# Last stage of an attention and expert-layer kernel: weight loads ahead of the wait for gathered rows, scatters at earlier counts, a small product ahead of a large one

## What is computed

```python
gates = softmax(h @ wg.T);  w_topk, idx_topk = top_k(gates, 8);  w_topk /= w_topk.sum(-1)
rank  = position of the assignment among those of its expert;  valid = rank < 160
buf[e, rank] = h[token]                                # 64 x 160 x 256
x1, x2 = split(buf @ expert_w1.T)                      # 2 x 768 columns
out   = (x1 * silu(x2)) @ expert_w2.T                  # 64 x 160 x 256
y     = where(valid, out[e, rank] * w_topk, 0)
combined = zeros.at[token].add(y)
x = x + gb * (shared_out + combined)
```

## Time and profile before

| | us |
|---|---|
| median of 3 runs | 1895.24 |
| lowest and highest | 1889.76, 1904.81 |
| the profiled execution | 1886.24 |
| its span, first to last instruction | 1884.5 |
| PE busy in the span | 1830.4 (97%) |
| DVE, ACT, POOL busy | 1232.2, 955.2, 945.7 |

### The profile page before, as it was taken

How to read it: one execution, slowest core, us unless ns; L and a number is a source line. 1 busy time by engine, 2 the same in 40 slices (tenths; PEclk the granted TensorE clock), 3 DMA queues, 4 the chain that set the end, 5 groups by cost and what they waited for, 6 DMA issues and landing times.

```text
span 1884.5 us, 36384 instructions
## 1 busy us (share of the span) xinstructions
PE 1830.4 (97%) x12428; PEld 1612.8 (86%) x12428; DVE 1232.2 (65%) x2454; ACT 955.2 (51%) x1789; POOL 945.7 (50%) x667
## 2 busy tenths in 40 slices
PE   7999999999999999999999999998999999999995
PEld 5888888888888888677888878898999999999994
DVE  8877777777777777666776668744555555555552
ACT  6666666666666665545453354333344444444341
POOL 5666566666666665025666656654333333323234
PEclk9999999999999999999999999999999999999998
DMA  6211111111111100302111002267888888888883
GB/s 228 68 38 38 34 37 34 34 37 34 37 34 47 41 31 21 130 20 69 45 46 46 20 25 66 68 207 236 280 288 284 291 283 262 285 290 283 284 280 86
DMA packets 141016, 234.08 MB, mean 124 GB/s; under 512 B 24756, under 2 KB 88971, under 8 KB 140816
## 3 DMA queue, kind: packets, MB, share of 16 engines
q1 hardware_dynamic: 116368, 220.50, 33.9%
q0 software_dynamic: 24576, 12.69, 4.5%
HBM read 194.58 MB, written 78.45 MB: 145 GB/s over the span
## 4 chain that ended last, share of the span: by engine, by line
PE 48%; DMA 6%; issue 2%; DVE 2%; POOL 1%; ACT 0%; POOLq 0%; SPq 0%; DVEq 0%; ACTq 0%
PE bank L85 24%; PE bank L1898 19%; DMA out_rows<-c_y_rest,c_token_rest 4%; PE bank L1165 4%; DMA c_w<-in_e1T 1%; POOL out_rows L2072 1%; PE bank L2120 1%; DMA slots<-last_row,last_index 1%; PE bank L1664 1%; POOL slots L1859 0%; DVE early L1543 0%; DVE b_h_low L1446 0%; ACT b_h_high L1343 0%; PE bank L2131 0%; DMA c_x<-slots 0%
## 5 line engine op out<-in xcount | busy, mean ns | idle before, releaser
L1898 PE MATMUL bank<-c_xT,c_w 128*128 128x160 f32 x3072 | 429.9, 299 | 6.1 <-DMA c_w<-in_e1T 5.4
L1898 PEld LDWEIGHTS bank<-c_xT,c_w 128*128 128x128 f32 x3072 | 419.3, 190 | 7.4 <-DMA c_w<-in_e1T 6.4
L1859 POOL DMA_INDIRECT slots<-b_row,b_index x224 | 249.5, 1114 | 199.8 <-issue 115.6
L2072 POOL DMA_INDIRECT out_rows<-c_y,c_x x64 | 100.0, 1563 | 377.6 <-DMA out_rows<-c_y_rest,c_token_rest 230.1
L2020 DVE TENSOR_TENSOR c_gT<-bank,c_sil 128x480 f32<-128x480 f32 x128 | 84.2, 658 | 220.5 <-PE bank L1898 220.5
L1988 ACT CAST c_gTs_high<-c_gT 128x384 fp32r<-128x384 f32 x128 | 65.5, 512 | 136.1 <-DVE c_gT L2020 136.1
L1981 ACT ACTIVATE c_sil<-bank 128x480 f32<-128x480 f32 x128 | 73.1, 571 | 113.1 <-PE bank L1898 113.1
L2013 DVE TENSOR_TENSOR c_gTs_low<-c_gT,c_gTs_high 128x384 fp32r<-128x384 f32 x128 | 71.6, 559 | 74.5 <-ACT c_gTs_high L1988 73.4
L454 POOL TENSOR_TENSOR last_row<-last_row,a_e 128x256 f32<-128x256 f32 x33 | 54.4, 1648 | 127.6 <-DVE a_e L710 125.9
L85 PE MATMUL bank<-c_w2s_high,c_gTs_high 128*128 128x256 f32 x384 | 115.3, 300 | 0.9 <-DVE c_gTs_low L2013 0.9
L85 PE MATMUL bank<-c_w2s_low,c_gTs_high 128*128 128x256 f32 x384 | 108.4, 282 | 0.0
(11 more groups left out here) (329 smaller groups left out, 5457.7 us busy)
## 6 DMA issues: line engine op xcount, KB each, us to landing
c_w<-in_e1T SPq DMA_DIRECT2D x64, 1536.0 KB, 7.0
c_w<-in_e2T SPq DMA_DIRECT2D x48, 768.0 KB, 8.8
early<-in_e2T SPq DMA_DIRECT2D x16, 768.0 KB, 8.8
slots<-a_fill SPq DMA_DIRECT2D x16, 642.0 KB, 3.7
c_x<-slots SPq DMA_DIRECT2D x64, 160.5 KB, 8.5
a_x_in<-in_x SPq DMA_DIRECT2D x32, 128.0 KB, 2.0
xT_tiles<-a_xT SPq DMA_DIRECT2D x32, 128.0 KB, 1.7
swaT_tiles<-a_swaT SPq DMA_DIRECT2D x32, 128.0 KB
```

The lines of the kernel that those rows point to most:

```text
L1859: pool.indirect_dma_start(out=T["slots"], out_offset=bass.IndirectOffsetOnAxis(ap=index[:, t, k:k + 1], axis=0), in_=row[:, t, :], in_offs ...
L1898: return nc.tensor.matmul(out, lhsT, rhs, start=first, stop=last, skip_group_check=True)
L2072: pool.indirect_dma_start(out=T["out"], out_offset=bass.IndirectOffsetOnAxis(ap=token, axis=0), in_=rows, in_offset=None, bounds_check=las ...
```

## The change

On SP, the first and second weights of the experts 2 to 7 (and the second weights of expert 1) are issued before the waits for `level{n}` and `held{n}`, and so ahead of these experts' rows. In the loop and the last eight steps the order stays. On POOL, levels 4 to 7 wait for other counts. On PE, `down_rest` goes ahead of `down` in the step, and gets the waits for `gT` and `w2_low` that it needs there. On DVE, `rest_rows` and `y_rows` of the very last step change places.

```diff
+        def load_weights(n, q):
+
+            sp.wait_ge(S("h_mm"), (n - 1) * 4)
+            load_w1(sp, n, q % 2)
+
         def step(n, q, i):
             first = isinstance(n, int) and n < RING
             if first:
+                if n >= 2:
+                    load_weights(n, q)
+                if n >= 1:
+                    load_w2(sp, n, q)
                 sp.wait_ge(B(f"level{n}"), 16 * TPC)
                 if n >= HELD:
                     sp.wait_ge(B(f"held{n}"), 16 * TPC)
...
-            if not first or n >= 2:
-
-                sp.wait_ge(S("h_mm"), (n - 1) * 4)
-                load_w1(sp, n, q % 2)
-            if not first or n >= 1:
-                if not first:
-                    wait_past(sp, S("rest_mm"), quad_of(q, i) - 1)
+            if not first:
+                load_weights(n, q)
+                wait_past(sp, S("rest_mm"), quad_of(q, i) - 1)
                 load_w2(sp, n, q)
...
         g_low(E - 1, RING - 1, 1)
+        rest_rows(E - QUAD, 1, QUADS, range(2, QUAD))
         y_rows(E - 1, RING - 1)
-        rest_rows(E - QUAD, 1, QUADS, range(2, QUAD))
...
-        level(4, "h_mm", 8)
-        level(5, "h_mm", 11)
-        held_level(6, "h_mm", 15)
-        level(6, "y_mm", 4)
-        held_level(7, "h_mm", 20)
-        level(7, "h_mm", 23)
+        level(4, "h_mm", 7)
+        level(5, "h_mm", 10)
+        held_level(6, "h_mm", 13)
+        level(6, "h_mm", 15)
+        held_level(7, "y_mm", 4)
+        level(7, "h_mm", 20)
...
             up(n, p, 0)
-            if late:
-                if static and n == 1:
-                    pe.wait_ge(B("base_raw"), 2 * CHUNKS)
-                down(n - 1, 1 - p)
+            if static and n == 1:
+                pe.wait_ge(B("base_raw"), 2 * CHUNKS)
             if q % QUAD == 0 and (not static or n >= QUAD):
+                pe.wait_ge(S("w2_low"), n)
+                pe.wait_ge(S("gT"), 2 * n)
                 down_rest((q // QUAD + 1) % 2, quad_of(q, i) - 1, range(QUAD))
             if static and n == E - 2:
+                pe.wait_ge(S("w2_low"), n)
+                pe.wait_ge(S("gT"), 2 * n)
                 down_rest(1, QUADS - 1, range(0, 2))
+            if late:
+                down(n - 1, 1 - p)
...
         up(E - 1, 1, 1)
+        pe.wait_ge(S("gT"), 2 * E)
+        pe.wait_ge(S("w2_low"), E)
+        down_rest(1, QUADS, range(2, QUAD))
         down(E - 1, 1)
-        down_rest(1, QUADS, range(2, QUAD))
```

## The result

Six runs of the changed kernel have the median 1920.15 us (1917.91 to 1923.42), six of the kernel before 1895.2 us (1887.69 to 1904.81). The forecast was +19 us, 1914.4, in a range of 1898 to 1926. The way and the place were right; the size was a quarter to a third short. The profiled execution took 1919.78 us.

The account below looks back on a forecast made before the run. PE was taken as the bound, waiting for weights and rows at the front; 15.8 + 0.4 + 3.0 = +19.2 us on the three runs' median of 1895.24 gave 1914.4 us, range 1898 to 1926.

Parts of the forecast that it names:

- The mechanism: Front, experts 2 to 7: gathered rows wait behind weights on SP's queue and PE stalls, 24.5 us in sum.
- What was removed: Front of the expert stage: 7.5 to 9.1 us of PE's waits to be had, taken as 8.7.
- The one stall forecast short: Expert 5: the product of rests (2.8 us) lies beside the wait for rows, so the stall is 1.4, say 1.5 us.
- The clock: PE after the front's long stalls: half clock costs 0.6 us each, +3.0 us; bounds 0 and 7.5.
- Rival (d): Front: clock falls for each stall's whole length and adds meet weights harder, +25.7 us, 1920.9 us; chance 0.14.
- Part 2: POOL's late scatters, levels 4 to 7, at smaller counts: they gate nothing once weights come first, 0 us.
- part 1: SP's weights ahead of the wait for the level: 24.5 us of stalls less 8.7 removed, +15.8 us.
- Part 3: PE's product of rests ahead of `down`: `y_rest` 0.4 us later in each group, +0.4 us once, no growth.
- rival (c): End of the kernel: POOL's chain sets it by itself though PE loses 19 us, +3 us, 1898.2 us; chance 0.07.
- Rival (b): Front: rows not held behind weights, landing about 3 us after issue; every stall goes, -8.3 us, 1886.9 us; chance 0.09.
- near 1327: Sign in the changed profile: expert 8's transposes begin near 1327 instead of 1311.5.

## Why the prediction was right, and where not

**The mechanism** was right, and shown by taking parts out: SP's part alone loses all of it, and with fewer bytes ahead of the rows the stalls shrink. Six waits of 25.3 us stand where five of 4.2 and one of 1.5 plus 2.0 for the adds were forecast, 24.5. That they agree so well is partly luck: expert 3, where no add runs yet, waited 5.4 us instead of 4.2, and expert 7, for which 1.5 us of adds were laid on top, waited 5.2; why expert 3's is long stays open. What was removed, 7.5 to 9.1 us, is gone. The one stall forecast short, at expert 5 beside the product of rests, is there with 1.09 us. The stalls alone give 25.3 - 7.5 = +17.8 us against 15.8.

**The clock was mis-sized.** The step that failed is "I take 0.6 each ... +3.0", and with it the bound of 7.5: I took the 1.5 us of the earlier trace rows as the most that one stall can cost. Of the 31.0 us lost at the front 17.8 are stalls, which leaves 13.2. Filling the stalls says about 13 too. And the granted clock says it directly: the earlier trace rows show half clock for 3.4 us, but at these stalls it lasted 6.83 us each time, five times, 34.1 us in all. Of that 6.9 us lay in the stalls themselves, as the prediction had thought possible, and 27.2 us on PE's work, the transposes and the 4 to 5 us of `up` behind them; half of it, 13.6 us, is lost. That is 2.6 to 2.7 us for each of the five long stalls, where 0.6 was taken and 1.5 was the bound. Rival (d), "the clock falls in each stall for its whole length", had the right event and the same wrong price. Its 1920.9 us stands beside the measured 1920.15 by luck: it takes some 6 us too little for the clock (7.5 against 13) and adds 2 for harder adds, which did not show as such. By the ratio, +29 us, the measured loss lies past its +25.7.

**Part 2 at 0** was right only because part 1 was there. By itself it is worth -6 us: the prediction said that rows can't go before t once weights are first, and it followed, but was not said, that with rows first the counts do most of what the change wanted. One reason that this was missed is that the prediction worked the loss of 5.4 us out at expert 2, where it is 0.57 us; 3.8 of it lie at the experts 6 and 7, whose levels were late.

**Part 3** was forecast at +0.4 with "no growth". In the changed kernel `y_rest` of the experts 56 to 59 ends at 1861.71, and POOL starts expert 56 at 1862.95 on a landing:

```profile
1859.36 0.48 DVE L2036 SCALAR_TENSOR_TENSOR c_y<-bank,c_x,mod 128x256 f32<-128x256 f32 x1 [1.55 <-PE bank L85]
1859.76 1.95 DVE L2044 SCALAR_TENSOR_TENSOR c_y_rest<-bank,c_x_rest,mod 32x256 f32<-32x256 f32 x4
```

DVE does `y` first and the rests behind it, as the prediction had it, and `y_rest` ends 2.55 us after the transposes ahead of it, before 2.11: 0.4 us later, as forecast. But the prediction left the loop as it was, and the loop grew by 0.8 us; and it did not see that `y_mm` also paces POOL, through level 6 with the old counts and held 7 with the new. POOL following PE was right in total: the 31 us of the front are all found at the end (rival (c) would have hidden them).

**Rival (b)**, rows not held, fell: PE had rows 7.9 to 9.3 us after their issue, not 3. The queue rule of the Trainium skill ("DMA: Bandwidth & Descriptors", section "Queues, rings and completion order") gave the right forecast. By the same section each DMA engine takes turns between its queues, a packet at a time. In the run with rows on POOL's queue they came sooner, as that would have it, but 6.4 and 6.6 us close behind weights is still long for 200 KB; no run here tells why.

**Thin readings.** The medians that the sum uses rest on fewer landings than issues: the 2.8 us of the earlier trace rows on two (3.15 and 2.38), the 8.6 us of the earlier trace rows on 12 of 31. Both stood up against PE's waits. And the forecast of expert 8's transposes "near 1327" holds the stalls alone (1311.5 + 15.8), without the 3.0 us for the clock.

## What to carry to other kernels

A small load that the next product waits for belongs ahead of a large one on the issuing engine's list, even if the large one is the one that was late: look for what held the large one (here a count on another engine) and move that. Price a new stall of PE with the half clock behind it, here 2.6 to 2.7 us on 4 to 5 us of idle, and take the length of the slow stretch from more than one event. Before a product is moved, list everyone who counts its semaphore, not only who reads its result.

## What the runs showed of the hardware

- The clock fell after idle stretches of very different length, and not every time after the same one. In the stage of the experts waits of 2.1 and 2.5 us left it at 1.00 in the kernel before, while each wait of 2.3 to 3.2 us with the second weights behind the rows was followed by 3.4 us at half rate, and each of 4.2 to 5.4 us in the changed kernel went with 6.8 us, which began before the wait was over. In the token stage PE waits 1.17 us for ACT, in the kernel with the rests first (until 1194.79) and in the kernel before (until 1192.30); the windows of 10 us around the end of this wait read

```profile
1192.00:1202.00 10.00, 8.37 (x46) 8.10 (x46) 8.32 (x15) 9.04 (x13) 7.47 (x7) 0.68 0.03 2
```

```profile
1189.00:1199.00 10.00, 7.75 (x61) 6.92 (x60) 9.17 (x17) 8.88 (x13) 6.74 (x6) 1.00 0.02 2
```

  with granted clocks of 0.68 (rests first) and 1.00 (before), on the same instructions. Eight of the fourteen profiles have this fall, and their expert stage begins some 3 us later than in the other six (1232.5 to 1234.8 against 1229.6 to 1231.4). It is not tied to one kernel's edit, and it moves a run by as much as several of the differences above. Among the 23 runs of the kernel before in the first set, the four with a mean granted clock of 0.994 and 0.995 took 1886 us, the four with 0.988 and 0.989 took 1893.
- Beside long rows of POOL's indirect DMAs, issued back to back, PE's own issue was slow: single matmuls came in steps of 0.7 us from about 12 us into a run of 32 scatters until 4 us behind its end, in both kernels that had such a run, and for 3 us after eight scatters and an add in a row, in both kernels that had that. Eight and twelve scatters in a row did it in no visible way in two others. Why is open. Late fetching of PE's instructions is a rival that no run tested: from 1230 to 1300 the instruction queue brought 16 KB at 1239.3 and at 1285.2 in the run with 32, and every 13 to 18 us with POOL's part alone. But PE and its weight loader did about as many instructions between two fetches in both (265 against 227 to 255), so the late fetch may follow from the slow issue as well as cause it.
- Scatters paced by counts, which look like idle time of POOL, are thus worth having here: without them PE stood 21.9 us with no releaser.
